# Attention samples reordered by pairs and layouts, with one bias sum and one row maximum over two PSUM banks

## The chip, the cores and the metric

One core of one Trainium2 chip runs the whole program. The metric is device time in microseconds for one execution. Five engines work side by side and are kept in order by semaphores: TensorE (PE: matrix products; its weight loads are listed apart as PEld), VectorE (DVE), ScalarE (ACT), GpSimd (POOL) and SyncE (SP: DMA queue). Each works through its own instruction list strictly as written. TensorE results land in PSUM, eight banks of 512 fp32 columns on each of 128 partitions; everything else is in SBUF.

## The reference

The input is x of 16 samples, 96 channels and a 16x16 image. Four layers follow each other, each as `x = x + layer(groupnorm(x))`. The first two are windowed attention over 8x8 windows, 12 heads:

```python
# layer 0: 12 heads of 8 channels, 4 windows of 64 tokens per sample
qkv = xw @ qkv_w.T + qkv_b
attn = softmax(einsum('bhnd,bhmd->bhnm', q * scale, k) + bias[h])     # bias per head, from a table
out = einsum('bhnm,bhmd->bhnd', attn, v) @ proj_w.T + proj_b

# layer 1: 12 heads of 32 channels, on the image rolled by (-4, -4)
dots = einsum('bhwid,bhwjd->bhwij', q, k) * scale + pos[rel]          # bias the same for all heads
dots = dots (+ masks of -inf in the last row and the last column of windows)
out = einsum('bhwij,bhwjd->bhwid', softmax(dots), v) @ w_out + b_out  # and rolled back by (4, 4)
```

Layer 2 is a quantized 3x3 depthwise and a 1x1 convolution, layer 3 a "spiking" attention with rounding. Neither is touched here. The group norm of a layer needs mean and variance of each sample of its input (32 groups of 3 channels over the image).

## The kernel before

Everything stays in SBUF after the load. The two attention layers (`L0` narrow, `L1` wide) are run by one generic body per engine, `pe_sample`, `act_sample`, `dve_sample` and `pool_sample`, called once per sample s by `attention_loop` (L1069 and on). Each body is an order written out by hand which mixes work of samples s-2 to s+2; the engines meet only through counted semaphores. Samples alternate between two sets of buffers.

A sample has 4 windows of 64 tokens, handled as 2 *pairs* j of windows; the 12 heads are 3 groups p of 4, of which one half u lies in partitions 0-63 and the other in 64-127. The work of a sample is:

- `act_norm` (L833): ACT writes the normalized sample into `xn`, tokens in window order: 2 pieces in L0, 5 in L1 (the roll cuts the windows).
- `pe_qkv` (L725, L733): products of `xn` with the weights into two PSUM banks in turn. L0 has three *uses* of a bank (q, k, v), L1 five (qk0, qk1, qk2, v0, v1). A use may be written only when the use before it in the same bank is evacuated. q and k are evacuated by ACT (L865/L871 one to three copies of q, L884/L888 two masked copies of k), v by DVE (L903) in four copies, since the product gives a window c in a partition half and the two heads h of a group have to go to two partition halves.
- `pe_scores` (L755): for a pair, 12 fp32 products (24 recorded) of 64x64 weights and 128 columns, into two banks, one for each head half u.
- `dve_scores` (L945, L947): for one half u of the pair, DVE adds the bias into `probs` and takes the row maxima. `pe_scores` of the next pair waits for both.
- `pool_shift` (L972): POOL subtracts the maximum. `pe_transpose` (L764, "T" below): 3 transposes into one bank; `act_exp` (L839): the exponential out of that bank into `probsT`, and only then may the next T write it.
- `pe_values` (L782): for a pair, 12 products with v, which carries a column of ones, so that the row sums come with it. `dve_heads` (L957, L959): reciprocal and product. `pe_turn` (L805), `act_heads` (L844/L847), `pe_out` (L819/L821), `act_out` (L854).
- `pool_residual` (L984): POOL adds into x, 2 pieces in L0, 5 in L1. `dve_new_x` (L587): statistics of the new x for the next layer's norm.

In the steady state TensorE's list for sample s is: scores (s,1), T (s,0), values (s-1,1), [L1: v0 of s+1], T (s,1), [L0: v; L1: v1 of s+1], turn, scores (s+1,0), T (s,2), values (s,0), [q of s+2; L1: qk0 and qk1 of s+2], out of s-1, T (s,3), [k of s+2; L1: qk2 of s+2], and in L1 a second turn. DVE takes the four units (one pair half each) of `dve_scores` between `dve_heads`, the v copies and the statistics:

```python
        def dve_sample(dve, L, s, prev, nxt, nxt2):
            for w in range(NW):
                if w < 2 or nxt:
                    dve_scores(dve, L, *at(s, w + 2))
                if w == 0 and prev:
                    dve_heads(dve, L, moved(s, -1), 1)
                if w == 2 and L.wide:
                    dve_heads(dve, L, s, 0)
                evacuate_step(dve, "dve", L, s, w, nxt, nxt2)
```

## Time and profile before

| | us |
|---|---|
| three runs | 583.41, 589.64, 594.77 |
| their median | 589.64 |
| the profiled execution | 589.08, span 587.1 |

The span is what the profile shows from the first to the last instruction; about 2 us of the run lie outside it. Layer 0 runs from about 47 to 210 us of the span, layer 1 from 210 to 470, then layers 2 and 3. The mean granted clock of TensorE is 0.921 of full speed. Rows of the timeline give start and duration in us, engine, line and operation, output<-input, count, and in brackets the idle time of that engine before it with what ended it. "x4" after a MATMUL counts recorded instructions; an fp32 product is recorded as two.

### The profile page before, as it was taken

The page shows a single profiled execution, that of the slowest core. Times are in us where ns is not written, and L with a number is a line of the kernel's source. Part 1 is how long each engine was busy: PE and PEld are TensorE (multiplying, and loading weights), DVE is VectorE, ACT ScalarE, POOL GpSimd, SP SyncE. Part 2 cuts the span into 40 slices and gives each one's busy share as a digit, 9 for nine tenths or more (in the row PEclk, how much of TensorE's full clock was granted, in tenths as well). Part 3 has the DMA queues.
Part 4 walks back from the last instruction along what each step waited for, and adds up shares of the span by engine and source line. Part 5 has one row for each costly group of instructions (what it writes and reads, how often), then busy time and mean ns, then how long its engine had stood idle before and what let it go on. Part 6 is the DMA issues. An engine that isn't in the chain of part 4 may idle for free.

```text
span 587.1 us, 13506 instructions
## 1 busy us (share of the span) xinstructions
PE 437.4 (75%) x4587; PEld 305.9 (52%) x4587; DVE 364.4 (62%) x882; ACT 268.5 (46%) x634; POOL 192.9 (33%) x310
## 2 busy tenths in 40 slices
PE   0665898898888787777777777787778788855664
PEld 0563676676666564555555555565556532223441
DVE  0883655665757754755555566666556489957784
ACT  0103454655566545554554445435554333145673
POOL 7021433534444541433332123333334334412212
PEclk9999777987899999999999899989999999967896
DMA  9400000000000000000000000000000000000001
GB/s 277 69 1 1 2 1 2 0 0 0 0 0 0 1 2 1 1 2 2 1 0 0 0 0 0 0 0 0 0 0 1 2 1 0 0 2 14 28 27 40
DMA packets 8509, 6.99 MB, mean 12 GB/s; under 512 B 5058, under 2 KB 8130, under 8 KB 8354
## 3 DMA queue, kind: packets, MB, share of 16 engines
q1 hardware_dynamic: 3984, 5.26, 3.0%
q10 hardware_dynamic: 4498, 1.38, 1.3%
q8 instruction: 16, 0.26, 0.2%
q14 instruction: 11, 0.09, 0.0%
HBM read 5.06 MB, written 1.57 MB: 11 GB/s over the span
## 4 chain that ended last, share of the span: by engine, by line
PE 41%; DVE 24%; issue 15%; ACT 11%; POOL 4%; DMA 3%; DVEq 1%; ACTq 1%; POOLq 1%
PE bank L725 9%; DVE v L903 7%; PE bank L755 6%; PE bank L764 6%; PE bank L782 5%; PE bank L819 4%; DVE probs L945 4%; DVE conv L1190 4%; PE bank L1271 3%; ACT q L871 3%; DMA table<-in_L_conv_rpb_table 3%; PE bank L733 2%; ACT k L884 2%; DVE stats L587 2%; PE bank L558 1%
## 5 line engine op out<-in xcount | busy, mean ns | idle before, releaser
L945 DVE TENSOR_TENSOR probs<-bank,bias 128x384 f32<-128x384 f32 x128 | 70.7, 553 | 126.7 <-PE bank L755 125.2
L839 ACT ACTIVATE probsT<-bank 128x384 f32<-128x384 f32 x128 | 62.7, 490 | 187.8 <-PE bank L764 187.8
L972 POOL TENSOR_TENSOR probs<-probs,row_max 128x384 f32<-128x384 f32 x128 | 105.9, 828 | 124.2 <-DVE row_max L947 123.5
L725 PE MATMUL bank<-xn,w 128*128 128x256 f32 x192 | 56.8, 424 | 49.5 <-DVE v L903 26.3
L984 POOL TENSOR_TENSOR x<-y_attn,x 96x64 f32 (+5 forms) x112 | 35.8, 337 | 157.1 <-ACT y_attn L854 157.1
L764 PE MATMUL bank<-cst,probs 128*128 128x128 f32 x384 | 71.9, 299 | 14.0 <-POOL probs L972 13.2
L947 DVE TENSOR_REDUCE row_max<-probs 128x6 f32<-128x384 f32 x128 | 70.8, 553 | 4.4
L755 PE MATMUL bank<-k,q 64*64 64x128 f32 x1536 | 62.1, 296 | 10.0 <-DVE probs L945 8.1
L725 PEld LDWEIGHTS bank<-xn,w 128*128 128x128 f32 x192 | 34.4, 198 | 63.9 <-DVE v L903 30.0
L764 PEld LDWEIGHTS bank<-cst,probs 128*128 128x128 f32 x384 | 46.4, 149 | 38.5 <-POOL probs L972 16.3
L903 DVE COPY v<-bank 64x192 f32<-64x192 f32 (+1 forms) x192 | 61.4, 320 | 4.5
L782 PE MATMUL bank<-v,probsT 128*64 128x18 f32 (+1 forms) x1536 | 61.3, 225 | 0.8 <-ACT probsT L839 0.8
L782 PEld LDWEIGHTS bank<-v,probsT 128*64 128x64 f32 x1536 | 53.5, 145 | 12.7 <-issue 11.4
L755 PEld LDWEIGHTS bank<-k,q 64*64 64x64 f32 x1536 | 45.8, 143 | 25.3 <-issue 25.2
L833 ACT ACTIVATE xn<-x,gn_shift,gn_rstd 96x64 f32 (+5 forms) x112 | 41.1, 438 | 20.3 <-DVE tapT L526 20.3
L884 ACT ACTIVATE k<-bank,cst 128x256 f32<-128x256 f32 x96 | 40.8, 489 | 0.0
L587 DVE BATCH_NORM_STATS2 stats<-x (+1 forms) x64 | 24.4, 415 | 12.2 <-POOL x L984 10.0
L1199 PE MATMUL bank<-pad,tapT 96*96 96x512 f32 x64 | 29.0, 595 | 1.6 <-ACT pad L1170 1.6
L725 PE MATMUL bank<-xn,w0T 128*128 128x256 f32 x64 | 26.4, 505 | 4.9 <-ACT xn L833 3.5
L1190 DVE SCALAR_TENSOR_TENSOR conv<-pad,dw_u,conv 96x512 f32<-96x512 f32 x32 | 28.6, 892 | 1.1
L819 PE MATMUL bank<-heads,p 128*96 128x256 f32 x96 | 28.3, 439 | 0.6 <-ACT heads L844 0.6
L1373 POOL TENSOR_TENSOR y_out<-y,x 96x512 f32<-96x512 f32 x8 | 10.6, 1323 | 53.3 <-ACT y L1366 53.3
(140 smaller groups left out, 598.8 us busy)
## 6 DMA issues: line engine op xcount, KB each, us to landing
rel_bc<-in_L_conv_rel_index SPq DMA_DIRECT2D x1, 2048.0 KB, 9.0
x<-in_x SPq DMA_DIRECT2D x4, 384.0 KB, 12.2
out_dram<-y_out SPq DMA_DIRECT2D x8, 192.0 KB, 2.1
w<-in_L_conv_w_qkv ACTq DMA_DIRECT2D x1, 432.0 KB, 5.1
cst<-in_consts ACTq DMA_DIRECT2D x1, 421.0 KB
p<-in_L_conv_w_out ACTq DMA_DIRECT2D x1, 144.0 KB, 5.0
pos<-in_L_conv_pos_emb SPq DMA_DIRECT2D x8, 2.0 KB
b_qk<-in_L_conv_qkv_b ACTq DMA_DIRECT2D x8, 0.1 KB, 6.9
```

The source lines that it names most:

```text
L725: last = nc.tensor.matmul(o[:, half * T:(half + 1) * T], w[:, col:col + 128], xn[par][:, :, :], start=True, stop=True)
L755: one = nc.tensor.matmul(ps_scores[u][c * WT:(c + 1) * WT, p * 128:(p + 1) * 128], q, k, start=True, stop=True)
L764: last = nc.tensor.transpose(ps_probsT[:, p * 128:(p + 1) * 128], probs[w][:, 2 * p:2 * p + 2, :], ident)
L782: last = nc.tensor.matmul(ps_heads[c * WT:(c + 1) * WT, at_:at_ + n], probsT[2 * j + u][:, p * 128 + c * WT:p * 128 + (c + 1) * WT], v, st ...
L819: last = nc.tensor.matmul(o, p1[:, p, :], heads1[parity(s)][:, p, :], start=(p == 0), stop=(p == NP - 1))
L839: nc.scalar.activation(probsT[w][:, :], ps_probsT[:, 0:NP * 128], ACT.Exp).then_inc(L.s.probsT_sb, 1)
L884: return nc.scalar.activation(dst, src, ACT.Copy, scale=scale)
L903: return nc.scalar.copy(dst, src) if eng == "act" else nc.vector.tensor_copy(dst, src)
L945: nc.vector.tensor_tensor(out, scores, b, ALU.add).then_inc(L.s.biased, 1)
L947: nc.vector.tensor_reduce(row_max[w][:, :], probs[w][:, :, :], AX.X, ALU.max).then_inc(L.s.maxed, 1)
L972: nc.gpsimd.tensor_tensor(probs[w][:, :, :], probs[w][:, :, :], by_row(row_max[w]), ALU.subtract).then_inc(L.s.shifted, 1)
L1190: ins = nc.vector.scalar_tensor_tensor(y, tap_of(par, t), dw_u[:, t:t + 1], y, ALU.mult, ALU.add)
```

## The change

1. **Layouts.** Windows are numbered by columns (windows 0 and 1 are the left half of the image). POOL's residual of layer 0 writes its result into a second tensor, `x_turned` (which lies where `rel_bc` was, no longer needed by then), already rolled as layer 1 wants it; the statistics of layer 1's norm read it. So `act_norm` is one operation of 96x256 in both layers. The residual has 4 pieces of 96x64 in both layers.
2. **v.** The product is made with one window's 64 tokens as weights (128x64) and the weight columns of one head half h, straight into the partition half where it is needed: 8 products of 48 columns in L0 (before: 2 of 96), 4 products of 192 columns per use in L1 (before: 1 of 384). DVE evacuates with 2 copies per use of 64x192 (L0) or 64x384 (L1); before, 4 of 64x96 or 64x192. All heads' v of L0 stay in one buffer by window.
3. **Order of the uses.** L0: q, v, k. L1: qk0, qk1, v0, qk2, v1.
4. **Pairs on DVE.** The two score banks are one tensor of [128, 2, 512]; bias sum and row maximum are one operation of 128x768 each per pair. `probs` and `row_max` are kept by pair; POOL's subtraction stays one operation per unit.
5. **The four bodies are written out anew.** `pe_out`, `act_out`, the residual and the statistics are those of sample s-2; values (s-1,1) come straight after scores (s,1), v straight after values; scores (s+1,0) come after T (s,1) and before values (s,0). ACT's masked k copies (L1: of qk2) are split around exp (s,1). After the last sample `pe_last`/`act_last` finish two outputs instead of one.

```diff
-        bank = [ctx.enter_context(nc.psum_tensor(f"bank{i}", [128, 512], F32)) for i in range(8)]
-        ps_scores = bank[0:2]
+        ps_scores = ctx.enter_context(nc.psum_tensor("ps_scores", [128, 2, 512], F32))
+        bank = [ps_scores[:, i, :] for i in range(2)]
+        bank += [ctx.enter_context(nc.psum_tensor(f"bank{i}", [128, 512], F32)) for i in range(2, 8)]
...
+        self.plan = [("qk", 0, 3), ("qk", 1, 3), ("v", 0, 2), ("qk", 2, 3), ("v", 1, 2)] if self.wide else \
+            [("q", 0, 3), ("v", 0, 2), ("k", 0, 2)]
...
-                for k in (range(NW // 2) if not L.wide else (j,)):
-                    at_ = 0 if L.wide else k * n
-                    last = nc.tensor.matmul(o[:, at_:at_ + n], xn[par][:, 2 * k:2 * k + 2, :].rearrange("c w t -> c (w t)"),
-                                            w1[:, 2 * n:3 * n] if L.wide else w0T[:, 256:], start=True, stop=True)
+                for at_, w in enumerate(windows):
+                    for h in range(NH):
+                        last = nc.tensor.matmul(o[h * WT:(h + 1) * WT, at_ * n:(at_ + 1) * n], xn[par][:, w * WT:(w + 1) * WT],
+                                                w_v[:, h], start=True, stop=True)
                 last.then_inc(L.s.v_ready, 1)
...
-            for of_image, of_tokens in window_pieces(L):
-                tokens = xn[parity(s)][0:C, :, :].rearrange("c w t -> c (w t)")
-                nc.scalar.activation(of_tokens(tokens), of_image(image(x_of(s))), ACT.Identity, bias=gn_shift[:, bass.ds(s * 1, 1)],
-                                     scale=gn_rstd[:, bass.ds(s * 1, 1)]).then_inc(L.s.xn_ready, 1)
+            src = x_in_of(L, s) if L.wide else windows_of_image(x_in_of(L, s))
+            dst = xn[parity(s)][0:C, :]
+            nc.scalar.activation(dst if L.wide else dst.rearrange("c (b y x) -> c b y x", b=2, x=WIN), src, ACT.Identity,
+                                 bias=gn_shift[:, bass.ds(s * 1, 1)],
+                                 scale=gn_rstd[:, bass.ds(s * 1, 1)]).then_inc(L.s.xn_ready, 1)
...
-        def dve_scores(dve, L, s, w):
-
-            dve.wait_ge(L.s.scores_ready, win_count(s, w))
+        def dve_scores(dve, L, s, j):
+
+            dve.wait_ge(L.s.scores_ready, win_count(s, 2 * j + 1))
...
             nc.vector.tensor_tensor(out, scores, b, ALU.add).then_inc(L.s.biased, 1)
-            dve.wait_ge(L.s.biased, win_count(s, w))
-            nc.vector.tensor_reduce(row_max[w][:, :], probs[w][:, :, :], AX.X, ALU.max).then_inc(L.s.maxed, 1)
+            dve.wait_ge(L.s.biased, pair_count(s, j))
+            nc.vector.tensor_reduce(row_max[j][:, :, :].rearrange("r u g -> r (u g)"),
+                                    probs[j][:, :, :, :].rearrange("r u g k -> r (u g) k"), AX.X, ALU.max).then_inc(L.s.maxed, 1)
...
         def pe_sample(pe, L, s, prev, nxt, nxt2):
...
+            pe_scores(pe, L, s, 1)
+            if prev:
+                pe_values(pe, L, moved(s, -1), 1)
+            if nxt:
+                pe_qkv(pe, L, moved(s, 1), L.v_index(0), L.v_index(0) + 1)
+            pe_transpose(pe, L, s, 0)
+            if nxt:
+                pe_qkv(pe, L, moved(s, 1), L.v_index(0) + 1, L.v_index(0) + 2)
+            if prev == 2:
+                pe_out(pe, L, moved(s, -2))
+            pe_transpose(pe, L, s, 1)
+            if prev and L.wide:
+                pe_turn(pe, L, moved(s, -1), 0)
+            if nxt:
+                pe_scores(pe, L, moved(s, 1), 0)
+            pe_values(pe, L, s, 0)
+            if nxt and L.wide:
+                pe_qkv(pe, L, moved(s, 1), L.v_index(1), L.v_index(1) + 1)
+            pe_transpose(pe, L, s, 2)
+            if nxt2:
+                pe_qkv(pe, L, moved(s, 2), 0, 1)
+            pe_transpose(pe, L, s, 3)
+            if nxt2 and L.wide:
+                pe_qkv(pe, L, moved(s, 2), 1, 2)
+            if prev:
+                pe_turn(pe, L, moved(s, -1), 1)
 
         def act_sample(act, L, s, prev, nxt, nxt2):
...
+            act_exp(act, L, s, 0)
+            if nxt:
+                evacuate(act, "act", L, moved(s, 1), late, 0, 1)
+            act_exp(act, L, s, 1)
+            if nxt:
+                evacuate(act, "act", L, moved(s, 1), late, 1)
+            if prev == 2:
+                act_out(act, L, moved(s, -2))
+            if nxt2:
+                act_norm(act, L, moved(s, 2))
+            if prev and L.wide:
+                act_heads(act, L, moved(s, -1), 0)
+            act_exp(act, L, s, 2)
+            if nxt2:
+                evacuate(act, "act", L, moved(s, 2), 0, 0, 1)
+            act_exp(act, L, s, 3)
+            if nxt2:
+                evacuate(act, "act", L, moved(s, 2), 0, 1)
+                if L.wide:
+                    evacuate(act, "act", L, moved(s, 2), 1)
+            if prev:
+                act_heads(act, L, moved(s, -1), 1)
 
         def dve_sample(dve, L, s, prev, nxt, nxt2):
...
+            dve_scores(dve, L, s, 1)
+            if prev:
+                dve_heads(dve, L, moved(s, -1), 1)
+            if nxt:
+                evacuate(dve, "dve", L, moved(s, 1), L.v_index(0))
+            if nxt:
+                dve_scores(dve, L, moved(s, 1), 0)
+            if L.wide:
+                dve_heads(dve, L, s, 0)
+                if nxt:
+                    evacuate(dve, "dve", L, moved(s, 1), L.v_index(1))
+            if prev == 2:
+                dve_new_x(dve, L, moved(s, -2))
 
         def pool_sample(pool, L, s, prev, nxt, nxt2):
...
+            for w in (2, 3):
+                pool_shift(pool, L, s, w)
+            if prev == 2:
+                pool_residual(pool, L, moved(s, -2))
+            if nxt:
+                for w in (0, 1):
+                    pool_shift(pool, L, moved(s, 1), w)
```

`late` is the use after the first v: k in L0, qk2 in L1. `evacuate(..., first, end)` issues the copies first to end of a use; a use of q or qk has the q copies first and the two k copies last.

## Rows read from the trace of the kernel before

**Rows 1.** Windows by stage: length, busy us (x count) per engine, clock, DMA
```profile
47.00:210.00 163.00, 134.34 (x1830) 103.40 (x1832) 100.74 (x246) 86.86 (x200) 65.24 (x94) 0.87 0.00 1
210.00:470.00 260.00, 203.25 (x2284) 147.07 (x2275) 149.23 (x361) 126.23 (x344) 80.47 (x154) 0.97 0.00 1
470.00:587.00 117.00, 80.38 (x310) 36.82 (x310) 87.88 (x194) 53.94 (x89) 32.59 (x30) 0.85 0.05 14
```

**Rows 2.** Timeline of one sample in layer 1, PE, ACT and DVE
```profile
299.60 1.13 PE L725 MATMUL bank<-xn,w 128*128 128x256 f32 x4 [1.79 <-DVE v L903]
300.57 1.46 PE L819 MATMUL bank<-heads,p 128*96 128x256 f32 x6
301.87 0.49 PE L764 MATMUL bank<-cst,probs 128*128 128x128 f32 x3
303.94 1.13 PE L725 MATMUL bank<-xn,w 128*128 128x256 f32 x4 [1.58 <-ACT k L884]
304.90 0.49 PE L805 MATMUL bank<-cst,headsN 128*128 128x128 f32 x3
305.33 0.89 PE L755 MATMUL bank<-k,q 64*64 64x128 f32 x24
306.14 0.55 PE L764 MATMUL bank<-cst,probs 128*128 128x128 f32 x3
306.26 0.56 DVE L945 TENSOR_TENSOR probs<-bank,bias 128x384 f32<-128x384 f32 x1 [5.54 <-PE bank L755]
306.62 0.92 PE L782 MATMUL bank<-v,probsT 128*64 128x66 f32 x24
306.73 0.49 ACT L839 ACTIVATE probsT<-bank 128x384 f32<-128x384 f32 x1 [0.81 <-PE bank L764]
306.86 0.55 DVE L947 TENSOR_REDUCE row_max<-probs 128x6 f32<-128x384 f32 x1
307.47 0.91 PE L733 MATMUL bank<-w,xn 128*128 128x384 f32 x2
307.59 0.23 DVE L957 RECIPROCAL inv_sum<-bank 128x12 f32<-128x12 f32 x1 [0.18 <-PE bank L782]
307.86 0.56 DVE L959 TENSOR_TENSOR headsN<-bank,inv_sum 128x384 f32<-128x384 f32 x1
308.22 0.49 PE L764 MATMUL bank<-cst,probs 128*128 128x128 f32 x3
...
314.59 1.13 PE L725 MATMUL bank<-xn,w 128*128 128x256 f32 x4 [1.70 <-DVE v L903]
```

**Rows 3.** Groups of instructions by line and shape: copies of v and k
```profile
L903 DVE COPY v<-bank 64x192 f32<-64x192 f32 x128 | 45.2, 353 | 3.0
L884 ACT ACTIVATE k<-bank,cst 128x256 f32<-128x256 f32 x96 | 40.8, 489 | 0.0
L888 ACT ACTIVATE k<-bank,b_k,cst 128x256 f32<-128x256 f32 x32 | 16.3, 571 | 0.0
L903 DVE COPY v<-bank 64x96 f32<-64x96 f32 x64 | 16.2, 253 | 1.5
```

**Rows 4.** Timeline of one sample in layer 0, TensorE
```profile
181.15 0.89 PE L755 MATMUL bank<-k,q 64*64 64x128 f32 x24
...
188.17 0.70 PE L725 MATMUL bank<-xn,w0T 128*128 128x256 f32 x2
188.70 0.59 PE L821 MATMUL bank<-heads,p0T 128*96 128x256 f32 x2
189.14 0.49 PE L764 MATMUL bank<-cst,probs 128*128 128x128 f32 x3
189.46 0.60 PE L725 MATMUL bank<-xn,w0T 128*128 128x256 f32 x2
189.99 0.89 PE L755 MATMUL bank<-k,q 64*64 64x128 f32 x24
```

**Rows 5.** Windows: two samples of layer 0 at the mixed clock
```profile
102.85:123.50 20.65, 17.72 (x243) 13.69 (x240) 12.81 (x31) 11.19 (x27) 8.19 (x12) 0.83 0.00 0
```

More of the change, by code:

```diff
@@ L724, in pe_qkv @@
                         col = half * (INNER if L.wide else 128) + j * 128
-                        last = nc.tensor.matmul(o[:, half * T:(half + 1) * T], w[:, col:col + 128], xn[par][:, :, :],
+                        last = nc.tensor.matmul(o[:, half * T:(half + 1) * T], w[:, col:col + 128], xn[par][:, :],
                                                 start=True, stop=True)
@@ L741, in pe_scores @@
             if j == 0:
-                for i in range(L.qk_uses):
+                for i in L.qk_indices():
                     evacuated(pe, L, s, i)
-            free = wait(pe, L.s.biased, win_count(s, 2 * j - 1))
+            free = wait(pe, L.s.biased, pair_count(s, j - 1))
             if free is not None:
@@ L820, in pe_out @@
             else:
-                last = nc.tensor.matmul(o, p0T[:, :], heads0[parity(s)][:, :], start=True, stop=True)
+                last = nc.tensor.matmul(o, p0T[:, :], image_of_windows(heads0[parity(s)][:, :]), start=True, stop=True)
             last.then_inc(L.s.out_ready, 1)
@@ L852, in act_out @@
             act.wait_ge(L.s.out_ready, s + 1)
-            wait(act, L.s.residual, s * L.adds)
+            wait(act, L.s.residual, s * 4)
             nc.scalar.activation(y_attn[:, :], ps_mix[0:C, 0:T], ACT.Identity,
@@ L1077, in pe_attention_norm, with pe_last, act_last @@
             pe_group_norm(pe, layer, half)
[L1081 to L1082 removed]
+        def pe_last(pe, L):
+            pe_out(pe, L, B - 2)
+            if L.wide:
+                pe_turn(pe, L, B - 1, 0)
+            pe_turn(pe, L, B - 1, 1)
+            pe_out(pe, L, B - 1)
+        def act_last(act, L):
+            act_out(act, L, B - 2)
+            if L.wide:
+                act_heads(act, L, B - 1, 0)
+            act_heads(act, L, B - 1, 1)
+            act_out(act, L, B - 1)
         def pe_first(pe, L, before):
             if before:
[L1087 to L1089 removed]
+                pe_values(pe, before, B - 1, 1)
+            last_qk = L.qk_indices()[-1] + 1
+            pe_qkv(pe, L, 0, 0, last_qk)
             if before:
[L1091 to L1092 removed]
+                pe_last(pe, before)
             pe_scores(pe, L, 0, 0)
[L1094 to L1101 removed]
+            pe_qkv(pe, L, 0, last_qk, len(L.plan))
+            pe_qkv(pe, L, 1, 0, L.ahead2)
         def act_first(act, L, before):
             act_norm(act, L, 0)
[L1105 removed]
+            for i in L.qk_indices():
+                evacuate(act, "act", L, 0, i)
             if before:
[L1107 removed]
+                act_last(act, before)
             act_norm(act, L, 1)
[L1109 to L1112 removed]
+            for i in range(L.ahead2):
+                evacuate(act, "act", L, 1, i)
         def dve_first(dve, L, before):
@@ L1518, in _ @@
             attention_loop(pool, L1, pool_sample, pool_group_norm)
-            for half in range(2):
-                pool_residual(pool, L1, B - 1, half)
+            for s in (B - 2, B - 1):
+                pool_residual(pool, L1, s)
             pair_loop(pool, pool_l2, norm_2, norm_3)
```

268 lines of the change are left out of this document (94 added, 174 removed).

## The prediction

> **What bounds the kernel now.** I read first the windows by stage [rows 1]: the two attention layers take 163 and 260 us of 587.1, and only they are changed; the 117 us behind them stay. TensorE is the busiest engine of both (134.34 of 163 us, 203.25 of 260), VectorE has 100.74 and 149.23, so no engine is full, and the question is what TensorE waits for. The timeline of one sample in layer 1 answers it [rows 2]. A sample's step is 314.59 - 299.60 = 14.99 us. TensorE stands idle twice in it: about 1.7 us until DVE's copies of v (L903) free the bank of the next q/k use, and 1.58 us until ACT's copies of k (L884) do. Together 3.3 us of 15.0. In layer 0 [rows 4] two scores groups a step apart stand at 181.15 and 189.99: a step of 8.84 us at full clock. Most of that stage ran slower: two steps took 20.65 us at a granted clock of 0.83 [rows 5], where two at full clock would be 17.68. So with 0.83 as a mean of the levels 1.2 and 2.4 GHz, a third of such a stretch is at 1.2 GHz, and it costs 2.97 us per two samples.
>
> **How the step is walked.** TensorE's new list is a chain: each group starts after the one before it, or when its semaphore comes. The time that a group occupies is the distance to the start of the next one [rows 2]: scores 0.81 (305.33 to 306.14), T before another mode 0.48 (306.14 to 306.62), values 0.85, v of 384 columns 0.75 (307.47 to 308.22), a q/k use 0.97 (299.60 to 300.57), out 1.30, turn 0.43. From layer 0 [rows 4]: T before a product 0.32, q or k 0.53, out 0.44. From scores to DVE's first sum 0.93; I take 1.03, since the pair needs the last product of both halves. From T to exp 0.59 (306.14 to 306.73), exp 0.49.
>
> **The pair operation on DVE.** One of 384 columns takes 0.55 to 0.56 [rows 2]. The copies of v show the slope: 96 columns 253 ns, 192 columns 353 ns [rows 3], so 100 ns more for 96 more, and the 384 of rows 2 lie on that line. Then 768 columns take 0.55 + 0.40 = 0.95 us, against 2 x 0.55 = 1.11 now. The bounds: 0.95 if two banks read as one, 1.11 if the second bank costs a new start. I take 0.95. Over 64 pairs and two operations DVE saves 64 x 2 x 0.155 = 20 us of busy time, but the maximum of the first half comes later: 1.9 us after the scores are ready instead of 1.1. In the new order the T that needs it stands behind values, v and (for T (s,2)) scores, so POOL's two subtractions are done before TensorE comes to it: no wait.
> The Trainium skill, page "VectorE: DVE Perf Modes", section on the TRN2 errata, gives VectorE 120 cycles plus one per column from PSUM and 58 from SBUF; an estimate from it for 768 columns is 0.93 and 0.86 us. The trace disagrees for 384 columns: 0.56 and 0.55 where the page would have 0.53 and 0.46. With the page's figures the layer 1 step below would be 0.12 us shorter, 2 us in all.
>
> **v on TensorE.** A use of L1 goes from one product of 384 columns to four of 192 in alternating halves of the output partitions, 768 columns. Bounds: by today's rate for a full-width product (0.75 us for 384) it takes 1.50; by the values group, which has the same 128x64 weights in alternating halves and 12 x 66 = 792 columns in 0.85 us [rows 2], it takes 0.82. The second is the same form, so I take 0.82, keep 1.50 as a rival. In layer 0 eight products of 48 columns: by count, 8 of the values group's 12, 0.55; at most 0.75. v follows values directly, both in the 64-wide form.
>
> **v copies on DVE.** Two of 64x384 (0.55 each by the line above) for four of 64x192 (0.353): 1.12 instead of 1.50 per use.
>
> **Layer 1, new step** (zero is the start of scores (s,1)): values 0.81, v0 1.66, T (s,0) 2.48, qk2 2.81, out 3.78, T (s,1) 5.08, turn 5.56, free at 5.99. Next is scores (s+1,0), which need both k copies of qk2, and these stand behind exp (s,1) on ACT: T 5.08 + 0.59 + 0.49 = 6.16, then 0.84 for two copies (these overlap; they stand at 489 ns each, rows 3): 7.02. So scores (s+1,0) start at 7.08, after 1.1 us of idling. Values 7.89, v1 8.74, T (s,2) 9.56, qk0 9.89, T (s,3) 10.86 (exp (s,2) is done at 10.64), ready for qk1 at 11.19. That one needs DVE's copies of v1, behind the pair sum, maximum and heads: 7.08 + 1.03 = 8.11, + 2 x 0.95 and the small gaps 10.08, heads 0.85 (0.23 + 0.56 and gaps) 10.93, v1 1.14: 12.1. So qk1 starts at 12.15, after 1.0 us of idling, turn 13.12, and the next scores (s+1,1) at 13.55. The two waits of 3.3 us have become two of 2.1, and ACT's norm, one piece instead of five, is off this path (ACT has some 8 us of work in 13.5). Gain 14.99 - 13.55 = 1.44 us per step. I count 13 full steps: 18.7 us. At 1.11 per pair operation it is 13.9, and the gain 14 us.
>
> **Layer 0, new step**: values 0.81, v 1.66, T 2.21, k 2.53, out 3.06, T (s,1) 3.50, exp done 4.58, second k copy 0.57 [rows 3] 5.17, scores (s+1,0) 5.23 (idle since 3.98), values 6.04, T (s,2) 6.89, q 7.21, T (s,3) waits for exp (s,2) till 8.02, turn 8.4, next scores 8.8. Against 8.84: nothing gained or lost. DVE's and POOL's work has gaps here. The residual has one piece more, and the statistics now come two samples late, behind the pair's maximum; nobody on the path waits for them inside the layer.
>
> **Ends.** At the seam of the layers the norm is 1 us shorter, and one more v and one more out stand ahead of the first scores, about 1.3 us: nothing. Behind the last sample of layer 1 two outputs remain instead of one, 1.30 + 0.43 and a copy: +2 us.
>
> **Sum.** 589.08 (profiled run) - 18.7 + 0 + 2 = 572.4 us. The median is 0.6 above the profiled run, so 573.
>
> **The rivals.**
> *v does not run in halves side by side.* Then v0 costs 1.50, the first part of the layer 1 step moves by 0.68, and DVE's chain with it: 14.2 per step, 8.8 us in all; layer 0 loses 0.2 x 14 = 2.8. Time 585. For it speaks that two products into alternating halves share all 128 weight rows; against it the values group, 792 columns in 0.85 us.
> The Trainium skill, page "TensorE: Matmul & The Clock Gate", "What overlaps and what doesn't", says that a weight load runs under a matmul only if it has other rows of the array; by that rule these would go one by one, and the trace's values group does not bear it out.
> *Layer 0 grows a wait.* ACT must be through with the last q copies and the heads of the sample before it reaches exp (s,0); I find 1 us of slack. If that goes, or the k copy comes late, each of 14 steps gets up to a further 1 us: 587.
> *Layer 0 keeps the full clock.* The stage has 0.87 [rows 1], which is 42 of 163 us at 1.2 GHz; at 2.97 per 7 us of it [rows 5] that is 18 us lost, two thirds of which lie in the steady steps. Before the clock fell TensorE had stood idle for over a microsecond at a time. If the new order's idling doesn't bring it down: 573 - 12 = 561.
> *The clock falls everywhere* (slower than before). The new waits of 1.1 to 1.3 us are single, and TensorE's work is the path on either side. If both layers run as rows 5 do, 17% over full clock, layer 1 (now 0.97) pays 1.9 us more for each of 14 steps and layer 0 some 5 us: 573 + 31 = 604. Slower than before from a mean clock of about 0.90 in layer 1 with layer 0 at 0.83. Against it: idling in layer 1 gets shorter, from 1.6 and 1.7 to 1.1 and 1.0 us, and it rarely brought the clock down.
>
> **How the numbers follow.** The forecast 0.50, own range 564 to 580 (the pair at 1.11: 578; two layer 1 steps in ten without their stretch at 1.2 GHz: 568); v one by one 0.15; the wait in layer 0 0.12; full clock 0.13; clock falls 0.10. About 2% (11.8 us) is what a measurement of this kernel can tell from no change, so faster means under 577.8 and slower over 601.4. Faster: 0.43 of the first, the 0.13 at full clock, 0.02 of the others: 0.58. Slower: 0.08, nearly all of the falling clock. The rest, 0.34, within 2%. The range 558 to 590 leaves out about a tenth on each side.
>
> **What would show it.** Right: bias sum and maximum x64 each at about 0.95 us; v copies of 64x384 at 0.55; scores groups of layer 1 one step apart at 13.5 us, with idle time before scores for ACT's k and before a q/k use for DVE's v, each about 1 us; layer 0 at 8.8 where the clock is full. Wrong: pair operations near 1.11; v groups of 1.5 us; idle time before T for POOL; a granted clock below 0.87 in layer 0 or 0.95 in layer 1. The walk takes every wait as the last semaphore plus 0.05 us; a wait that I overlooked in either order would break it first.

## The result

| | median | runs | profiled run | its span | its clock |
|---|---|---|---|---|---|
| before | 590.37 us | 4, 583.41 to 594.77 | 589.08 us | 587.1 us | .921 |
| after | 542.21 us | 4, 535.90 to 545.63 | 545.63 us | 543.8 us | .936 |

The kernel after takes 0.9185 of the time before, 95% interval 0.9042 to 0.9327: faster by 8%. In a second measurement (run 9) it took 545.56 us (542.03 to 547.60) where the kernel before took 592.66. The forecast was 573 and its range ended at 558: the direction was right, the size was missed by 31 us, more than half of the gain. The profiled execution of the kernel after is the slowest of its four; a second profile of the same kernel (run 9 below) has each of the seven stretches that follow within 1.3 us.

**Where the 43.3 us between the two spans are.** The 64 groups of scores (TensorE, L755) are the same work in both kernels, 32 in each layer, so the starts of the same group cut both spans at the same places. The windows between the starts of groups 1, 5, 29 (layer 0, L0), 33, 37, 61, 64 (layer 1, L1) and the end, for the kernel after (us from:to, length, busy us and count of PE, PEld, DVE, ACT and POOL, granted clock, DMA share, GB/s):

```profile
52.71:71.32 18.61, 13.85 (x205) 10.18 (x205) 11.92 (x22) 8.85 (x19) 8.52 (x11) 1.00 0.01 2
71.32:180.75 109.43, 92.60 (x1585) 72.23 (x1585) 63.76 (x107) 65.81 (x144) 51.42 (x92) 0.94 0.00 1
180.75:217.25 36.50, 29.58 (x329) 22.36 (x329) 14.62 (x29) 14.33 (x34) 12.91 (x27) 0.72 0.01 1
217.25:238.69 21.44, 16.78 (x224) 12.42 (x224) 15.29 (x30) 11.16 (x28) 9.84 (x16) 1.00 0.01 2
238.69:395.54 156.85, 133.95 (x1776) 104.29 (x1777) 91.65 (x155) 81.46 (x205) 51.43 (x92) 1.00 0.00 0
395.54:413.06 17.52, 14.96 (x216) 11.72 (x216) 12.16 (x27) 8.07 (x21) 8.91 (x17) 1.00 0.01 2
413.06:543.80 130.74, 91.30 (x449) 45.09 (x448) 93.05 (x205) 59.22 (x101) 36.32 (x40) 0.87 0.04 13
```

And the same seven of the kernel before:

```profile
51.85:74.07 22.22, 18.08 (x186) 13.33 (x186) 13.03 (x34) 9.47 (x22) 7.96 (x11) 0.85 0.01 2
74.07:194.99 120.92, 102.74 (x1441) 79.85 (x1441) 75.88 (x180) 67.13 (x157) 49.06 (x72) 0.86 0.00 0
194.99:224.46 29.47, 22.49 (x306) 16.79 (x306) 15.58 (x41) 15.42 (x40) 12.03 (x18) 0.94 0.01 1
224.46:249.78 25.32, 19.29 (x207) 13.08 (x206) 18.39 (x47) 12.79 (x36) 8.70 (x13) 1.00 0.01 1
249.78:434.98 185.20, 145.58 (x1634) 106.36 (x1633) 105.50 (x252) 91.64 (x253) 54.63 (x108) 0.97 0.00 0
434.98:456.64 21.66, 16.50 (x203) 12.17 (x202) 16.30 (x44) 9.43 (x25) 9.14 (x17) 1.00 0.00 1
456.64:587.10 130.46, 91.26 (x439) 44.51 (x439) 93.14 (x206) 57.73 (x97) 36.77 (x40) 0.85 0.04 13
```

Line by line: the start of L0 -3.6 us, its 12 steady steps -11.5, the seam of the layers **+7.0**, the start of L1 -3.9, its 12 steady steps -28.35, its end -4.1, everything behind +0.3; group 1 itself starts 0.9 later. The clock column moves too: 12 steps of L0 from 0.86 to 0.94, of L1 from 0.97 to 1.00, the seam from 0.94 to 0.72, the start of L0 from 0.85 to 1.00.

**A step of L1 after**, the timeline (start, us, engine, line, operation, idle time before it and what ended it), to be held against [rows 2]. The rows of TensorE and VectorE, without VectorE's statistics; of ScalarE only the two that scores wait for:

```profile
304.01 0.89 PE L755 MATMUL ps_scores<-k,q 64*64 64x128 f32 x24 [1.17 <-ACT k L885]
304.82 0.92 PE L782 MATMUL bank<-v,probsT 128*64 128x66 f32 x24
305.07 0.96 DVE L938 TENSOR_TENSOR probs<-ps_scores,bias 128x768 f32<-128x768 f32 x1 [3.20 <-PE ps_scores L755]
305.58 0.82 PE L733 MATMUL bank<-w,xn 128*64 128x192 f32 x8
306.06 0.95 DVE L940 TENSOR_REDUCE row_max<-probs 128x12 f32<-128x768 f32 x1
306.33 0.55 PE L764 MATMUL bank<-cst,probs 128*128 128x128 f32 x3
306.71 1.03 PE L723 MATMUL bank<-xn,w 128*128 128x256 f32 x4
306.93 0.22 DVE L951 RECIPROCAL inv_sum<-bank 128x12 f32<-128x12 f32 x1
307.19 0.56 DVE L953 TENSOR_TENSOR headsN<-bank,inv_sum 128x384 f32<-128x384 f32 x1
307.58 0.49 PE L764 MATMUL bank<-cst,probs 128*128 128x128 f32 x3
307.66 1.13 DVE L901 COPY v<-bank 64x384 f32<-64x384 f32 x2
308.85 1.13 PE L723 MATMUL bank<-xn,w 128*128 128x256 f32 x4 [0.78 <-DVE v L901]
309.81 0.49 PE L805 MATMUL bank<-cst,headsN 128*128 128x128 f32 x3
310.23 0.89 PE L755 MATMUL ps_scores<-k,q 64*64 64x128 f32 x24
...
315.62 0.49 ACT L840 ACTIVATE probsT<-bank 128x384 f32<-128x384 f32 x1 [1.24 <-PE bank L764]
316.01 0.83 ACT L885 ACTIVATE k<-bank,cst 128x256 f32<-128x256 f32 x2
...
317.09 0.67 PE L755 MATMUL ps_scores<-k,q 64*64 64x128 f32 x16 [1.17 <-ACT k L885]
```

The step is 317.09 - 304.01 = 13.08 us, where the steady ones before were 14.99 ([rows 2]) and 15.08 in turn at full clock, 15.04 on average. The two waits are those of the prediction: for ACT's k, 1.17 us, and for DVE's v behind sum, maximum and heads, 0.78 us. Together 1.95 instead of 3.3.

**L0 after**, from the timeline of TensorE over two half steps:

```profile
93.89 0.65 PE L733 MATMUL bank<-w0T,xn 128*64 128x48 f32 x16
94.47 0.55 PE L764 MATMUL bank<-cst,probs 128*128 128x128 f32 x3
...
97.51 0.89 PE L755 MATMUL ps_scores<-k,q 64*64 64x128 f32 x24 [1.22 <-ACT k L889]
...
99.13 0.87 PE L764 MATMUL bank<-cst,probs 128*128 128x128 f32 x3
```

The 1.22 us of idling for ACT's k are the 1.25 predicted. At 99.13 the same T takes 0.87 us that took 0.55 at 94.47: here the clock has fallen to 1.2 GHz. Steps that keep 2.4 GHz take 8.67 and about 8.82 us in turn (the loop holds two samples), those in which it falls 9.88 to 9.92. So at full clock a step takes 8.74 on average: the 12 steps of run 5 below, which are alike, took 104.87 us at 1.00. Before, they were 8.84 and 8.93 in turn, on average 8.88 (run 3).

### The profile page after: what moved, and what is told of

The parts are those of the page before. It is cut to its first block, busy times and chain, and to the rows that moved or that the text cites. A ratio compares the mean times of both kernels' runs of the same rounds, so it can differ in the third digit from the quotient of the medians.

```text
span 543.8 us, 13840 instructions
## 1 busy us (share of the span) xinstructions
PE 415.9 (76%) x4971; PEld 298.9 (55%) x4971; DVE 329.8 (61%) x658; ACT 253.6 (47%) x554; POOL 194.0 (36%) x326
## 4 chain that ended last, share of the span: by engine, by line
PE 59%; DVE 14%; ACT 10%; issue 9%; DMA 3%; POOL 1%; ACTq 1%; DVEq 1%; POOLq 0%
PE ps_scores L755 11%; PE bank L723 10%; PE bank L764 10%; PE bank L782 9%; PE bank L733 5%; DVE conv L1204 4%; PE bank L819 4%; PE ps_scores L1285 3%; DMA table<-in_L_conv_rpb_table 3%; ACT k L885 2%; ACT probsT L840 2%; DVE v L901 2%; ACT k L889 2%; PE bank L805 2%; PE bank L564 2%
## 5 line engine op out<-in xcount | busy, mean ns | idle before, releaser
L938 DVE TENSOR_TENSOR probs<-ps_scores,bias 128x768 f32<-128x768 f32 x64 | 61.3, 958 | 132.5 <-PE ps_scores L755 132.0
L755 PE MATMUL ps_scores<-k,q 64*64 64x128 f32 x1536 | 60.7, 291 | 37.6 <-ACT k L889 19.6
L755 PEld LDWEIGHTS ps_scores<-k,q 64*64 64x64 f32 x1536 | 45.6, 141 | 51.5 <-issue 49.5
L940 DVE TENSOR_REDUCE row_max<-probs 128x12 f32<-128x768 f32 x64 | 61.0, 953 | 2.2
L723 PE MATMUL bank<-xn,w 128*128 128x256 f32 x192 | 52.4, 398 | 11.9 <-DVE v L901 11.5
L901 DVE COPY v<-bank 64x384 f32<-64x384 f32 (+1 forms) x96 | 46.4, 483 | 8.0 <-PE bank L733 6.5
L978 POOL TENSOR_TENSOR x<-y_attn,rel_bc 96x96 f32 (+3 forms) x64 | 18.4, 316 | 40.1 <-ACT y_attn L855 40.1
L866 ACT ACTIVATE q<-bank 128x256 f32<-128x256 f32 x48 | 18.4, 384 | 25.6 <-PE bank L723 25.6
L1213 PE MATMUL ps_scores<-pad,tapT 96*96 96x512 f32 x64 | 29.0, 595 | 1.6 <-ACT pad L1184 1.6
L872 ACT ACTIVATE q<-bank,b_q,cst 128x256 f32<-128x256 f32 x48 | 25.1, 563 | 5.4 <-PE bank L723 5.3
L733 PE MATMUL bank<-w,xn 128*64 128x192 f32 x256 | 26.4, 327 | 0.0
```

Source lines behind the costliest of these rows:

```text
L723: last = nc.tensor.matmul(o[:, half * T:(half + 1) * T], w[:, col:col + 128], xn[par][:, :], start=True, stop=True)
L733: last = nc.tensor.matmul(o[h * WT:(h + 1) * WT, at_ * n:(at_ + 1) * n], xn[par][:, w * WT:(w + 1) * WT], w_v[:, h], start=True, stop=True)
L755: one = nc.tensor.matmul(ps_scores[c * WT:(c + 1) * WT, u, p * 128:(p + 1) * 128], q, k, start=True, stop=True)
L901: return nc.scalar.copy(dst, src) if eng == "act" else nc.vector.tensor_copy(dst, src)
L938: nc.vector.tensor_tensor(out, scores, b, ALU.add).then_inc(L.s.biased, 1)
L940: nc.vector.tensor_reduce(row_max[j][:, :, :].rearrange("r u g -> r (u g)"), probs[j][:, :, :, :].rearrange("r u g k -> r (u g) k"), AX.X, ...
```

## The experiments

Each is named by a number. "12 steps" is the window from the 5th to the 29th group (L0) or from the 37th to the 61st (L1).

**1, 2. The pair operations and the v copies, each undone in the kernel after.**

```
-            nc.vector.tensor_tensor(out, scores, b, ALU.add).then_inc(L.s.biased, 1)
+            for u in range(NU):
+                nc.vector.tensor_tensor(out[:, u], scores[:, u], b[:, u], ALU.add).then_inc(L.s.biased, 1)
```

The maximum is cut in the same way, and POOL's subtractions still wait for both halves.

> The changed kernel with the pair operations taken apart again: two bias sums of 128x384, then two row maxima of 128x384 for each pair; POOL still waits for both. My theory: DVE's operations of a pair lie on the path only in layer 1, where the next q/k use waits for the v copies behind them. Four operations of 0.55 take about 0.35 us more than two of 0.95, so layer 1's step goes from 13.07 to about 13.4 us and layer 0's stays at 8.67; some 4 us in all. Rival: the pair operation carries the main part of the 48 us, then steps of layer 1 come back to 14 us or more, or layer 0's grows.

It took 551.05 us. The L1 step became 13.20 us, 0.13 longer, not 0.35; the L0 steps stayed 8.67 and some 8.86 in turn. The timeline of DVE in it says why:

```profile
307.72 1.02 DVE L939 TENSOR_TENSOR probs<-ps_scores,bias 128x384 f32<-128x384 f32 x2 [3.08 <-PE ps_scores L755]
308.77 1.01 DVE L942 TENSOR_REDUCE row_max<-probs 128x6 f32<-128x384 f32 x2
```

Two operations of 384 columns in a row, neither of which waits for the other, take 1.02 us together, not 2 x 0.55: the second begins before the first has ended. So 768 columns in one operation (0.96) gain 0.06 us each over two such ones. The 0.155 that the prediction took per operation is the difference to two that stand apart, as they did before [rows 2], where the maximum waited for the sum of its own half.

```
-                todo = [lambda h=h: evac_v(who, L, s, i, j, h) for h in range(NH)]
+                todo = [lambda c=c, h=h: evac_v(who, L, s, i, j, c, h) for c in range(2) for h in range(NH)]
```

Each copy takes half the columns, and the counts of the uses are raised to four.

> The changed kernel with v evacuated in four copies of half the width instead of two per use. Same place on the path as the pair operation: layer 1's step 13.07 to about 13.45 us (four copies 1.50 us for 1.13), layer 0 unchanged at 8.67. Rival (v copies are off the path in the new order): 13.07 stays.

551.22 us; the L1 step 13.45 (as expected), the L0 step unchanged. The 0.38 us of the four copies lie in full on the L1 step: its second wait is for them. So the copies are worth three times what the pair operations are. Runs 1, 2 and 4 were executed once each, and not together with the kernel after: their whole times, all about 551, lie further from 542.21 than the steps explain, and part of that lies where the clock fell (run 1: the seam 38.15 us at 0.64 instead of 36.50 at 0.72). They are read by their steps.

**3. Does the idling bring down the clock of L0?** The kernel before, with four products that nobody reads where TensorE would stand still ahead of T(s,1):

```
+            wait(pe, L.s.probsT_sb, win_count(s, w - 1))
+            if w == 1 and not L.wide:
+                for _ in range(4):
+                    nc.tensor.matmul(ps_probsT[:, 0:128], ident, w0T[:, 0:128], start=True, stop=True)
             pe.wait_ge(L.s.shifted, win_count(s, w))
-            wait(pe, L.s.probsT_sb, win_count(s, w - 1))
```

> The kernel before, with four products of 128x128 by 128 columns that nobody reads put into TensorE's idle time ahead of the second transpose of each layer 0 sample (about 1.0 of the 1.2 us that it waits for POOL). Theory A, it is TensorE's idling that brings the clock down in layer 0: the granted clock of that stage goes from 0.87 to 0.97 or more, the steps stay at 8.84 us but hardly any takes 11.8, 12 steps go from 121 to about 107 us and the run is some 10 us faster, although TensorE does more. Theory B, the clock falls for another reason: it stays at 0.87 or below, and the extra products make the run the same or slower.

It took 579.44 us (574.79 to 585.22) against 591.49, a ratio of 0.9842 (0.9747 to 0.9938): work added, time gained. Its 12 steps of L0:

```profile
77.06:183.63 106.57, 99.95 (x1537) 80.19 (x1537) 75.88 (x180) 67.24 (x158) 48.33 (x71) 1.00 0.00 0
```

106.57 us at 1.00, where the kernel before has 120.92 at 0.86. The step is 106.57 / 12 = 8.88: steps of 8.84, as in [rows 4], and of 8.93 in turn. So the 14 us over full clock in L0 before came of TensorE's idling. Why the kernel after loses less is not shown: at full clock a step idles 1.17 us for POOL and 0.38 for DVE before, 1.22 for ACT's k and some 0.3 for its exp after. In this run L1, which has no such products and is as before, took 180.14 us for its 12 steps at 1.00, where the profile of before has 185.20 at 0.97. The Trainium skill, "TensorE: Matmul & The Clock Gate", Part 1, has a monitor that gates TensorE's clock by how busy the engine has been; by that rule, the run agrees. The mean busy share of a stretch doesn't order the clocks, though: before, TensorE was busy for 102.74 of 120.92 us in L0's 12 steps at 0.86 and for 145.58 of 185.20 in L1's at 0.97.

**4. The order of the v products.** The half of the output partitions outside, the window inside, so that they no longer alternate:

```
-                for at_, w in enumerate(windows):
-                    for h in range(NH):
+                for h in range(NH):
+                    for at_, w in enumerate(windows):
```

> The changed kernel with the products of v issued all for one partition half first, then all for the other, instead of alternating. Theory: alternating halves run side by side, so without that a v group of layer 1 takes 1.2 to 1.5 us instead of 0.75 and the step goes from 13.07 to about 13.6 us (the first v shifts the path, the second falls into the wait for DVE). Rival: they never ran side by side, the group stays at 0.75.

550.98 us. The groups of v in its timeline, one of L0 and one of L1:

```profile
126.36 0.92 PE L733 MATMUL bank<-w0T,xn 128*64 128x48 f32 x16
127.20 0.55 PE L764 MATMUL bank<-cst,probs 128*128 128x128 f32 x3
...
298.11 0.87 PE L733 MATMUL bank<-w,xn 128*64 128x192 f32 x8
298.91 0.55 PE L764 MATMUL bank<-cst,probs 128*128 128x128 f32 x3
```

In L1 the group occupies 0.80 us (298.11 to 298.91) where it had 0.75 (305.58 to 306.33), not 1.5; the step is 13.12: the expected 13.6 was a miss. In L0, with 48 columns, it occupies 0.84 instead of 0.58, and the steps are 8.93 and 9.09 in turn, some 0.27 longer. So only the short products of L0 gain much from alternating halves. In L1 it is not the alternation that makes 768 columns cost as little as the 384 of before: half by half they take 0.80 and not 1.5. What does is not shown. The Trainium skill, "TensorE: Matmul & The Clock Gate", "What overlaps and what doesn't", lets a weight load run under a product only in other rows of the array, which all of these share; the group of L1 shows hardly any such price.

**5 to 8. What the walk says is left.** The prediction's walk names what ends each wait, so it can be used further. In the kernel after, the out of a sample (1.30) stands ahead of T(s,1), on whose exp ACT's k copies wait; and DVE's heads stand ahead of the v copies that TensorE waits for. Run 5 moves the first, run 6 the second, run 7 both:

```
+            pe_transpose(pe, L, s, 1)
             if prev == 2:
                 pe_out(pe, L, moved(s, -2))
-            pe_transpose(pe, L, s, 1)
...
-                dve_heads(dve, L, s, 0)
                 if nxt:
                     evacuate(dve, "dve", L, moved(s, 1), L.v_index(1))
+                dve_heads(dve, L, s, 0)
```

> The changed kernel with TensorE's transpose of (s,1) issued before the out product of sample s-2 instead of behind it. My theory of the new step: the next scores wait for exp (s,1) and ACT's two k copies behind it, counted from that transpose. It comes 1.3 us earlier in layer 1 and 0.44 in layer 0, and out fills the wait. Layer 1 from 13.07 to 11.9 us a step, layer 0 from 8.67 to 8.25. Rival (ACT itself is the bound, its queue is full): the scores come no earlier, the idle time of 1.2 us only moves.

> The changed kernel with DVE's v1 copies of layer 1 issued before the heads of (s,0). Theory: the second wait of the layer 1 step, 0.78 us before the last q/k use, is for these copies, which stand behind 0.8 us of heads that nobody needs before the next sample: step 13.07 to 12.3 us, layer 0 unchanged at 8.67. Rival: the turn or the next values then wait for the heads and the step stays above 12.8.

> Both of the two reorderings. If the two waits are independent, their gains add: layer 1 at 11.1 us a step, no idle time of TensorE above 0.2 us left in it, layer 0 at 8.25. If one hides the other: 11.9.

(5) took 526.69 us: L1 step 11.92, as the walk has it. L0 stayed at 8.67 and 8.82 in turn where 8.25 was expected: a miss. There T(s,1) is not held up by the out but by exp (s,0): it starts 1.30 us behind T(s,0) in both kernels (95.77 - 94.47 after, 133.93 - 132.63 in run 5), and the chain exp, T, exp, k on ACT and TensorE sets the half step. (6) took 543.72: L1 step 12.35, as expected, but of the 11 us that this is worth in 15.5 steps the whole shows next to nothing, since the clock was lower elsewhere (the start of L0 21.40 us at 0.84 instead of 18.61 at 1.00, the seam 38.96 at 0.65, the end 133.32 at 0.84). Both together 519.97: L1 step 11.20, that of L0 as in run 5. Each of the three was executed once.
The eighth moves values (s,0) of L0 into the gap ahead of scores (s+1,0), and a turn ahead of T(s,3), on top of both:

```
+            if not L.wide:
+                pe_values(pe, L, s, 0)
             if nxt:
                 pe_scores(pe, L, moved(s, 1), 0)
-            pe_values(pe, L, s, 0)
+            if L.wide:
+                pe_values(pe, L, s, 0)
```

> Both reorderings, and in layer 0 values (s,0) before scores (s+1,0) and the turn before the transpose (s,3), so that they fill the waits for ACT's k copy and for exp (s,2). By the walk: layer 0 from 8.25 to 7.8 us a step, layer 1 as with both (11.1). Together with the clock as it was that is 542 - 12 - 26 = about 504 us. With TensorE idling less, the clock should stay up in layer 0 (0.98 or more in the steady steps) if idling is what brings it down; if it is load that brings it down, it falls below 0.95 there.

It took 506.69 us (505.54 to 512.29), 0.8632 of the kernel before (0.8561 to 0.8703): far below the kernel after, too, which was measured at other times. Its 12 steps of L0, the seam, and the 12 steps of L1:

```profile
72.92:170.79 97.87, 89.65 (x1587) 68.55 (x1585) 63.75 (x107) 65.55 (x144) 51.41 (x92) 0.98 0.00 1
170.79:201.26 30.47, 23.53 (x307) 17.62 (x305) 14.62 (x29) 13.78 (x33) 12.91 (x27) 0.89 0.01 1
222.69:356.99 134.30, 133.96 (x1776) 102.78 (x1777) 91.73 (x155) 81.52 (x204) 51.42 (x92) 1.00 0.00 0
```

By the profile L1 is full: 133.96 us of PE in 134.30. The L0 steps are 8.22 and 7.88 in turn, 8.05 on average, not the 7.8 expected: TensorE now waits for exp in two places, 0.32 us each in the longer step, as its timeline shows:

```profile
144.72 0.52 PE L764 MATMUL bank<-cst,probs 128*128 128x128 f32 x3 [0.32 <-ACT probsT L840]
145.07 0.60 PE L821 MATMUL bank<-heads,p0T 128*96 128x256 f32 x2
145.99 0.88 PE L782 MATMUL bank<-v,probsT 128*64 128x18 f32 x24 [0.32 <-ACT probsT L840]
```

**9 to 11. The order against the smaller operations.** The kernel after once more; the kernel after with the pair operations, the two v copies and the norm in one piece all undone; and with the norm alone in four pieces.

```
+            for n in range(4):
...
+                nc.scalar.activation(piece, of, ACT.Identity, bias=gn_shift[:, bass.ds(s * 1, 1)],
+                                     scale=gn_rstd[:, bass.ds(s * 1, 1)]).then_inc(L.s.xn_ready, 1)
```

> The changed kernel unaltered, beside the others of this call. Steps as before, 13.07 us in layer 1 and 8.67 in layer 0 at full clock; if its clock in layer 0 or 1 differs from the first time, the steps there differ by just that. About 542 us.

> The changed kernel with three parts undone together: bias sum and row maximum as two operations each, four v copies per use, and the norm in four pieces instead of one. What is left is the new order with the v product in halves. Theory: the costs add on the path of layer 1 only, 0.13 for the operations, 0.37 for the copies, nothing for the norm: 13.6 us a step, layer 0 stays at 8.67, so about 7 us over the changed kernel, 549. So most of the gain of 48 us is the order's. Rival: the smaller operations together fill DVE or ACT and the steps go back to 14.5 or more.

> The changed kernel with only the norm in four pieces of 64 columns (about 1.4 us of ScalarE instead of 0.6). ScalarE has a gap of more than a microsecond behind it in both layers, so both steps stay: 8.67 and 13.07 us. Rival: it pushes the exponential behind it and with that the transpose (s,3), at least 0.3 us a step.

Kernel after 545.56 (542.03 to 547.60); order alone 553.31 (549.14 to 556.89); norm in pieces 545.12. Steps of L1: 13.08, 13.50, 13.07; of L0, where the clock is full, 8.67 and some 8.83 in turn for the kernel after and the norm in pieces, 8.53 and 8.86 for the order alone. So of the 47 us between 592.66 and 545.56, 39 belong to the new order with the v products in its layout, and 8 to everything that the change makes into fewer operations, most of that in the v copies (0.38 x 15.5 = 5.9, run 2). The 39 are between medians of a kernel before that took 581.83 to 596.48 us here; by the steps of L1, the order makes 1.54 of the 1.96 us. The norm in one piece is worth nothing.

**12. The same products that nobody reads, in the L0 loop of the kernel after**, ahead of scores (s+1,0):

```
             if j == 0:
+                if not L.wide and not isinstance(s, int):
+                    wait(pe, L.s.biased, pair_count(s, j - 1))
+                    for _ in range(4):
+                        nc.tensor.matmul(ps_scores[:, 0, 0:128], ident, w0T[:, 0:128], start=True, stop=True)
```

> The changed kernel with four products of 128 columns that nobody reads in the idle time before scores (s+1,0) of layer 0's loop (1.07 of 1.2 us). If idling brings the clock down, it stays at 2.4 GHz there: the 12 steps take 104 us (12 x 8.67) instead of 109.4, with 8.67 unchanged per step. If load brings it down, the clock falls more often than in the unaltered one beside it.

It took 545.47 us, no less. The 12 steps took 105.77 us, where 104 was expected and run 9 has 110.73. The eleven behind the first, and the seam:

```profile
83.23:177.99 94.76, 89.60 (x1541) 72.83 (x1541) 58.76 (x99) 60.48 (x133) 48.24 (x88) 1.00 0.00 0
177.99:216.93 38.94, 32.02 (x328) 24.41 (x329) 14.62 (x29) 14.47 (x34) 12.93 (x27) 0.65 0.00 1
```

The same eleven steps of run 9, the kernel after:

```profile
81.78:182.63 100.85, 85.41 (x1452) 66.56 (x1453) 58.75 (x99) 60.72 (x134) 48.27 (x88) 0.93 0.00 0
```

In the steps the clock stays up and six microseconds come back, but the seam behind them is 2.4 us longer, at 0.65, and the first step of the loop ran slow (11.01 us). Not all six are the clock: the filled steps are 8.53 and 8.71 in turn, 0.13 shorter at full clock, which was not expected. The idling of the L0 steps costs the kernel after some 5 us (100.85 less 11 x 8.74, or 109.43 less the 104.87 of run 5); what a single run wins by filling them depends on where the next fall comes.

**13, 14. Is the seam's loss the clock or the work?** In the kernel after TensorE stands still for 1.62 us in the seam, and the clock falls behind it (the timeline; the v group of L0 has 0.65 at full clock above and 0.97 here). The kernel before stood still for 1.86 us ahead of the same group norm, and its v group behind it kept the 0.58 us of full clock, so the length of this one wait does not explain the fall. After and before:

```profile
186.03 0.31 PE L638 MATMUL bank<-gn_in,cst 96*96 96x16 f32 x2 [1.62 <-DVE gn_in L614]
...
187.81 0.97 PE L733 MATMUL bank<-w0T,xn 128*64 128x48 f32 x16
```

```profile
200.85 0.34 PE L632 MATMUL bank<-gn_in,cst 96*96 96x16 f32 x2 [1.86 <-ACT y_attn L854]
...
203.61 0.58 PE L733 MATMUL bank<-w0T,xn 128*128 128x96 f32 x4
```

Runs 13 and 14 put products that nobody reads ahead of the waits there; `fill(pe, n)` issues n of them, of 128x128 weights and 128 columns. Two of the places:

```
+                if layer == 1:
+                    pe.wait_ge(L0.s.biased, pair_count(B - 2, 0))
+                    fill(pe, 6)
                 pe.wait_ge((L0, L1)[layer - 1].s.y_ready, B - 4)
...
+            if before:
+                fill(pe, 4)
             pe_qkv(pe, L, 0, 0, last_qk)
```

> The kernel after with products that nobody reads ahead of TensorE's waits at the seam between the layers (6 before the group norm of layer 1, 4 before the first products of layer 1, 3 before T(15,1) and T(15,3), 4 before the scores of (15,0)). The seam, from the 29th to the 33rd group of scores, took 36.50 us at a granted clock of 0.72 in the kernel after and 29.47 at 0.94 before. Theory A, the clock falls there because TensorE idles in the seam, and the fall is what the 7 us are: the clock stays near 1.0 and the seam takes 28 to 30 us, the whole 7 us less than the kernel after. Theory B, the 7 us are the work that now stands at the seam (one more turn and output, their waits): the clock is up and the seam still takes 33 us or more. If the clock is down in spite of the products, the run tells neither.

> The kernel of e8_both_and_layer0 (506.69 us) with the same unread products at the seam. Its seam took 30.47 us at a granted clock of 0.89. Theory A (the seam is lengthened by the clock): about 27 us there and 503 for the whole. Theory B (the work sets it): 506 to 508, since the added products are in the way.

Run 13 took 541.43 us. Its seam in the windows:

```profile
180.28:210.41 30.13, 25.84 (x368) 20.99 (x368) 14.62 (x29) 14.03 (x34) 12.87 (x27) 1.00 0.01 1
```

30.13 us at 1.00 instead of 36.50 at 0.72, just outside the 28 to 30 expected of the clock and far from the 33 expected of the work. So 6.4 us of the seam after are the clock. Unfilled runs agree: 34.82 us at 0.80 in run 2, 36.53 at 0.72 in run 9, 38.96 at 0.65 in run 6. The seam before paid for its 0.94 as well, an estimated 1.5 us at the rate of [rows 5] (2.97 per 7 us at 1.2 GHz), so of the 7.0 us that the seam lost some 5 to 6.4 are the clock, and 0.7 to 2.2 the additional work that stands there. The whole did not get 7 us shorter: the start of L0 and the end ran at 0.91 and 0.84 in this one execution (19.23 and 133.29 us). In run 14, the kernel of 8 with the same products, the seam takes 30.14 us at 1.00 against 30.47 at 0.89, and the whole 504.77 (504.59 to 509.31) against 506.69 (505.54 to 512.29) on another chip: no difference that these runs can tell. There the stretch at 1.2 GHz cost almost nothing, or the products took what it gave back; the two runs don't tell which.

## Why the prediction was wrong

Its sum had -18.7 for L1, 0 for L0, 0 for the seam and +2 for the end, -16.7 in all; the spans have -43.3. Two steps failed above all: L1's term was right in kind and half the size, and L0's clock, worth 9.8 us, stood in the sum at nothing. Term by term:

**L1, -18.7 predicted, -36.4 measured** (232.18 us from group 33 to group 64 before, 195.81 after). The mechanism was right: both waits are where the walk has them, for the reasons it gives. Three things were mis-sized. The step gained 15.04 - 13.07 = 1.97 us, not 1.44. The half with out is 0.21 shorter than walked (310.23 to 317.09, 6.86 us, against 7.08): values ahead of v occupy 0.75, not 0.85, v 0.75, not 0.82, a q/k use behind a T 0.86, not the 0.97 taken from behind other work. The half with the wait for v is 0.25 shorter (6.22 against 6.47), since DVE's own chain is: the pair operations with their gaps take 0.08 less, the heads 0.73 and not 0.85. In 13 steps the 0.53 us that the walk missed are 6.9 us. Then the number of steps: from group 33 to group 64 there are 31 half steps, 15.5 steps, and the first and last gain like the others: 2.5 x 1.97 = 4.9 us. And L1's clock: 12 steps before took 185.20 us where 12 x 15.04 is 180.5, so 4.7 us went to short stretches at 1.2 GHz; after, there are none. The prediction had them as 5 us in its own range and at nothing in its sum. Together 16.5 of the 17.7 missing. These 4.7 are in part luck: run 3, whose L1 is that of before, had none either (180.14), while all profiles of the kernel after and its variants have L1's 12 steps at 1.00.

**L0, 0 predicted, -15.1 measured.** The step at full clock is 8.74 on average, close to the 8.8 of the walk, against 8.88: 1.7 us in 12 steps (106.57 in run 3, 104.87 in run 5, both at 1.00). The rest is the clock. The 12 steps before stand 14.35 us over full clock, after 4.56: 9.8 us. The start of the layer took 3.6 us less with the clock at 1.00 instead of 0.85; between 0.9 and 2.8 of it is where the clock happened to be down, for runs 5 to 7, with the same work there, took 21.40, 21.40 and 19.47 us at 0.84 to 0.85. This was a rival, "layer 0 keeps the full clock", and it came true by two thirds; it stood at 0.13. The step that failed is that its likeliest case kept L0's clock at what it was, while the walk itself put one wait of 1.25 us in the place of the former waits. Run 3 shows how much hung on it. Why the new waits let the clock fall less often, the runs leave open. How often the new order would let the clock fall could not be read from the profile of before; that it should go into the range as a gain of 12 us and into the main case with more than nothing could.

**The seam, 0 predicted, +7.0 measured.** The work was judged at nothing and is 0.7 to 2.2 us (run 13); the clock, most of the 7.0, was not judged at all. The prediction followed the clock in the steady steps alone. The profile of before had a wait of 1.86 us there and kept the clock behind it, so it gave no sign of the fall.

**The end, +2 predicted, +0.3 measured.** The second output is there, but the time from the last group of scores to the end is 130.74 us at 0.87 against 130.46 at 0.85. Runs of the kernel after and its variants in which that stretch had 0.84 or 0.85 took 132.6 to 133.4, so the 2 us may be there and hidden by the clock.

**The pair operation** was predicted at 0.95 and took 0.958 (sum) and 0.953 us (maximum), the first bound: two banks read as one. The Trainium skill, "VectorE: DVE Perf Modes", the section on the TRN2 errata, has besides the table that the prediction drew on a measured rule for adding fp32 tensors, columns plus 151 cycles, from which an estimate for the sum is 957 ns; its row agrees with that rule and not with the table. For a maximum the page states no such rule; 953 is near the same figure. But what it is worth was judged wrong: 18.7 less 13.9, 4.8 us, between the pair operation at 0.95 and at 1.11 (two operations of 0.16 in 13 steps are 4.2); in run 1 undoing it costs 0.13 us per step, some 2 us in 15.5 steps. The v copies took 0.550 as predicted. The groups of instructions of the kernel after (busy us, mean ns of one, idle time before):

```profile
L938 DVE TENSOR_TENSOR probs<-ps_scores,bias 128x768 f32<-128x768 f32 x64 | 61.3, 958 | 132.5 <-PE ps_scores L755 132.0
L940 DVE TENSOR_REDUCE row_max<-probs 128x12 f32<-128x768 f32 x64 | 61.0, 953 | 2.2
L901 DVE COPY v<-bank 64x384 f32<-64x384 f32 x64 | 35.2, 550 | 4.4 <-PE bank L733 3.4
```

**The rivals.** v one by one fell with the 0.75 us of the group itself; but what spoke against it, products in alternating halves side by side, is not the reason in L1, where run 4 took the alternation away and paid 0.05. The wait in L0 did not come: its step is 0.14 shorter. That the clock falls everywhere is contradicted by L1 at 1.00. Over the whole, the clock made some 9 to 12 of the 43 us between these two executions: 9.8 and 0.9 to 2.8 in L0 and 4.7 in L1, less 5 to 6.4 at the seam. Only the 9.8 and the seam's rest on runs with and without idling; the others come and go from one execution to the next.

## What to carry to other kernels

A chain walked group by group from the timeline finds the right waits and, walked on, the next improvements: runs 5 to 8 took off another 36 us (542.21 to 506.69) with moves of a few lines, and the walk had the L1 step of runs 5 to 7 right to 0.1 us. That of L0 it missed, by 0.5 us in run 5 and 0.25 in run 8, where TensorE waits for exp. Take each group's length from the same neighbour that it will have, count steps by one marker from end to end, and price an operation merged out of two against two that run under each other, not against two that wait. Where the granted clock is under 1.00, put it into the sum as a term of its own, with its place: what the clock did was a quarter of the gain here and nearly all of it in L0, and one run with products that nobody reads measures it.

## What was not expected of the hardware

- Added work made a kernel faster: four 128x128x128 products per step of L0 took 120.92 us down to 106.57 (run 3), and twenty at the seam took it from 36.50 to 30.13 (run 13).
- An idle time of 1.22 us per step in L0 let the clock fall now and then (0.94), one of 1.17 and one of 0.78 us per step in L1 did not in any profile (1.00).
- Two VectorE operations of 384 columns that don't depend on each other take 1.02 us back to back, where a single one takes 0.55.
- A wait of 1.86 us ahead of a group norm left the clock up in the kernel before, one of 1.62 at the same place in the kernel after was followed by its fall.
- Eight matmul records of 64 output partitions by 192 columns occupy TensorE for 0.75 us when the halves alternate and 0.80 when they don't; with 48 columns and sixteen records 0.58 and 0.84.
